# Layer 0's output projection and row norm moved into its closing step and the first MLP product; layer 1's closing step reordered

## The reference, cut to what matters

```python
# layer 0: 16 heads of 32
qn, kn, vn = LN(x, ln1), LN(ctx, ln1), LN(ctx, ln1)
out = softmax((qn @ wq + bq) (kn @ wk + bk)^T / sqrt(32)) (vn @ wv + bv)
x1  = x + out @ wo + bo
x2  = x1 + gelu(LN(x1, ln2) @ w1 + b1) @ w2 + b2          # w1: 512 x 2048
# layer 1: 16 heads of 64
out = softmax((x2 @ Wq / 8) (ctx @ Wk)^T - 2) (ctx @ Wv)
y   = LN(out @ Wfc + x2, gamma, beta)
```

## Time and profile before

| | |
|---|---|
| median of 3 runs | 1577.0 us (1571.5 to 1578.2) |
| the profiled execution | 1579.7 us, span 1577.9 us |
| TensorE (PE) busy | 1398.7 us, 89% |
| VectorE (DVE) busy | 872.8 us, 55% |
| ScalarE (ACT) busy | 694.1 us, 44% |
| GpSimd (POOL) busy | 503.5 us, 32% |
| mean granted TensorE clock | 0.951 of full |

### The profile page before, as it was taken

The page is one execution under the profiler, slowest core; times in us unless marked ns, Lnnn a source line. Parts: engine busy times, 40 slices in busy tenths (PEclk is TensorE's granted clock), DMA queues, the critical chain, the costliest instruction groups (busy, mean ns, idle before and its releaser), DMA issues. The chain is left out here.

```text
span 1577.9 us, 31349 instructions
## 1 busy us (share of the span) xinstructions
PE 1398.7 (89%) x12780; PEld 876.5 (56%) x12780; DVE 872.8 (55%) x1550; ACT 694.1 (44%) x1328; POOL 503.5 (32%) x529
## 2 busy tenths in 40 slices
PE   3864998898989856799999999999999999999996
PEld 2432565565556542454455666666666666666653
DVE  5754677677676538552343445544555555546554
ACT  4442566665565543431212444444444444444431
POOL 4701566566565657002000121111112122121122
PEclk9996999999999858899999999999999999999998
DMA  6334443443433204302344232323232232323320
GB/s 197 100 73 99 91 121 99 101 110 101 118 82 85 56 16 148 120 1 92 110 149 87 65 102 59 103 65 103 49 90 67 46 95 65 103 65 85 92 69 29
DMA packets 123985, 138.32 MB, mean 88 GB/s; under 512 B 57282, under 2 KB 99778, under 8 KB 121794
## 3 DMA queue, kind: packets, MB, share of 16 engines
q1 hardware_dynamic: 123842, 136.33, 32.6%
HBM read 61.73 MB, written 20.87 MB: 52 GB/s over the span
## 5 line engine op out<-in xcount | busy, mean ns | idle before, releaser
L608 POOL TENSOR_TENSOR attn_probs<-attn_p,attn_probs 128x400 f16<-128x400 f32 (+1 forms) x288 | 284.4, 994 | 869.9 <-ACT attn_probs L1124 866.7
L1320 DVE TENSOR_REDUCE attn_nmax<-attn_p_max 100x1 f32<-100x722 f32 x256 | 231.9, 906 | 201.9 <-PE attn_p_max L875 200.0
L858 PE MATMUL attn_p_proj<-kv_w_v,attn_ctxT 128*128 128x512 f16 (+1 forms) x1152 | 264.3, 379 | 1.1 <-DVE attn_vbuf L1359 1.1
L853 PE MATMUL attn_p_proj<-attn_ctxT,kv_w_k 128*128 128x361 f16 x1536 | 249.1, 317 | 4.1 <-DVE attn_knat L1353 3.5
L1114 ACT ACTIVATE attn_p<-attn_p_sc,attn_score_bias 128x400 f32<-128x400 f32 x192 | 113.7, 592 | 312.0 <-PE attn_p_sc L904 312.0
L1124 ACT CAST attn_probs<-attn_p 128x400 f16<-128x400 f32 (+1 forms) x384 | 197.6, 517 | 0.0
L853 PEld LDWEIGHTS attn_p_proj<-attn_ctxT,kv_w_k 128*128 128x128 f16 x1536 | 144.5, 97 | 88.7 <-DVE attn_knat L1353 9.7
L1114 ACT ACTIVATE attn_p<-attn_p_sc 128x400 f32<-128x400 f32 x192 | 96.5, 503 | 189.5 <-PE attn_p_sc L900 179.1
L858 PEld LDWEIGHTS attn_p_proj<-kv_w_v,attn_ctxT 128*128 128x128 f16 (+1 forms) x1152 | 110.3, 101 | 112.4 <-DVE attn_vbuf L1359 1.4
L858 PE MATMUL attn_p_proj<-l_w_v,attn_ctxT 128*128 128x512 f16 (+1 forms) x576 | 142.2, 400 | 0.2 <-DVE attn_kscaled L1349 0.2
L853 PE MATMUL attn_p_proj<-attn_ctxT,l_w_k 128*128 128x361 f16 x768 | 131.6, 323 | 2.1 <-DVE attn_kscaled L1349 1.9
(11 more groups left out here) (199 smaller groups left out, 2497.2 us busy)
## 6 DMA issues: line engine op xcount, KB each, us to landing
kv_w<-attn_knat SPq DMA_DIRECT2D x128, 180.5 KB, 3.4
attn_kstack<-attn_knat SPq DMA_DIRECT2D x192, 90.2 KB, 2.2
ctx_turned<-attn_ctxT SPq DMA_DIRECT2D x8, 1444.0 KB, 8.8
attn_ctxT<-ctx_turned SPq DMA_DIRECT2D x8, 1444.0 KB, 7.7
attn_kstack_b<-attn_knat SPq DMA_DIRECT2D x64, 180.5 KB, 3.6
attn_c<-in_ctx_dram SPq DMA_DIRECT2D x40, 256.0 KB
rows_wo_w<-in_L_xattn_w_dram SPq DMA_DIRECT2D x8, 512.0 KB, 3.6
cols_w_w<-in_L_xattn_w_dram SPq DMA_DIRECT2D x4, 1024.0 KB, 5.6
```

The source lines that it names most:

```text
L608: eng.tensor_tensor(probs[:r, g % 2, 1, t, :HG * SQ], p32[:r, t % 3, :], probs[:r, g % 2, 0, t, :HG * SQ], ALU.subtract).then_inc(p_lo_mad ...
L853: last = pe.matmul(bank[:, :HALF], w_k[:, wa, k, c0 + m * P:c0 + (m + 1) * P], ctxT[:, cpar, ca, k, n * HALF:(n + 1) * HALF], **flags)
L858: last = pe.matmul(bank[:r, :], ctxT[:, cpar, ca, k, P * t:P * t + r], w_v[:, wa, k, c0:c0 + E], **flags)
L1320: dve.tensor_reduce(nmax[:SQ, hh:hh + 1], p_max[:SQ, :, :HALF], AX.XY, ALU.max, negate=True).then_inc(max_made, 1)
```

## The change

- Tiles are cut alike everywhere: five of 128 rows, one of 60, one of 100 (`ROW0`, `RROWS`).
- `wo` is loaded and split one step earlier, in step 7 of layer 0; the first 512 columns of `w1` are split in the closing step into `w_first` (the room of layer 0's key weights).
- In the closing step and the tail the first five tiles go through the output projection and the row norm: `row_products` in slots 1, 7, 13, 19, 25 counted from the closing step's start, `row_sum` three slots later, then scale, shift, hi, lo, turn, one slot each. Their sums x1 are stored to memory. In the closing step the lo part of the probabilities is made by GpSimd and DVE in turn.
- `rows_stage("rows_wo")` and `columns_stage` are gone. `mlp_up` does the Gelu product with all blocks for rows 0 to 399 first, and tiles 5 and 6 on the way.
- In layer 1, `Wfc` is split in slots 4, 5, 10 and 11; `close_rows` takes slots 0 to 9; GpSimd takes the power of tile 5 in slot 9, behind `out_lo`. The first product waits for all but one of the projections to be read, the second tile for the last.

```diff
-        self.close = {1 + i: divmod(i, 2) for i in range(10)} if layer == 1 else {}
+        self.close = {i: divmod(i, 2) for i in range(10)} if layer == 1 else {}
+        self.next = [11, 12, 13, 14] if layer == 0 else [4, 5, 10, 11]
+        self.row_acc, self.row_sum, self.row_scale, self.row_add, self.row_hi, self.row_lo, self.row_turn = 1, 4, 5, 6, 7, 8, 9
+    def row_tile(self, s, j, ahead):
+        T, rest = divmod((s - self.units) * self.n + j - ahead, KT)
+        return T if self.layer == 0 and rest == 0 and 0 <= T < EARLY else None
...
 # attention, SP, layer 0
+                    if u == U - 1:
+                        sp.wait_ge(proj_ready, NPROJ * u)
+                        sp.wait_ge(ctxT_moved[0], 16 * (B // 2))
+                        load_next_weight(0)
                     stack_k(u, u % 2, 0)
...
+                for dst, vector, sem in zip((bo_row, g2_row, b2_row), mid_vectors, (bo_loaded, g2_loaded, b2_loaded)):
+                    sp.dma_start(dst, vector.partition_broadcast(P)).then_inc(sem, 16)
+                sp.wait_ge(next_lo_made, ET)
+                for T in range(EARLY):
+                    sp.dma_start(mid[T], x_d[ROW0[T]:ROW0[T] + P, :]).then_inc(mid_loaded[T], 16)
                 sp.wait_ge(proj_ready, NPROJ * U)
-                load_next_weight(0)
+                load_next_weight(1)
...
+                for T in range(EARLY):
+                    sp.wait_ge(mid_summed, T + 1)
+                    sp.dma_start(x1_d[ROW0[T]:ROW0[T] + P, :], mid[T]).then_inc(mid_stored, 16)
...
 # attention, TensorE
+            def row_products(T):
+                r0, r = ROW0[T], RROWS[T]
...
+                for k in range(ET):
+                    for i, (a, b) in enumerate(PARTS):
+                        last = pe.matmul(p_proj[:r, T % 2, :], outT[0][:, a, k, r0:r0 + r], next_weights[0][1 + b][:, k, :],
+                                         start=(k + i == 0), stop=(k == ET - 1 and i == 2))
+                last.then_inc(mid_ready, 1)
...
             def close_rows(T, half):
...
                 if T == 0 and half == 0:
                     pe.wait_ge(next_lo_made, ET * len(next_weights))
-                    pe.wait_ge(proj_freed, NPROJ * U)
+                    pe.wait_ge(proj_freed, NPROJ * U - 1)
...
+                if T == 1 and half == 0:
+                    pe.wait_ge(proj_freed, NPROJ * U)
...
 # attention, DVE
+            def row_sum(T):
...
+                dve.scalar_tensor_tensor(mid[T][:r], p_proj[:r, T % 2, :], 1.0 / WS, mid[T][:r], ALU.mult, ALU.add).then_inc(mid_summed, 1)
...
+                dve.bn_stats(stats[:r, T % 2, :], mid[T][:r]).then_inc(mid_stats_made, 1)
...
+                dve.bn_aggr(mv[:r, T, :], stats[:r, T % 2, :]).then_inc(mid_mv_made, 1)
...
+                dve.tensor_scalar(mid_rstd[:r, T:T + 1], mv[:r, T, 1:2], eps, None, ALU.add).then_inc(mid_var_made, 1)
...
+                dve.scalar_tensor_tensor(mid_z[T % 2][:r], mid[T][:r], mv[:r, T, 0:1], g2_row[:r], ALU.subtract, ALU.mult).then_inc(mid_centred, 1)
...
-                    if layer == 1 and has_scores and j > 0 and (t - 1) % 2:
+                    if (layer == 1 or s == U) and has_scores and j > 0 and (t - 1) % 2:
...
 # attention, GpSimd
-                    if layer == 1 and s == U + 1 and j == PV_T + HG:
+                    if layer == 1 and s == U + 1 and j == sl.out_t:
                         row_rstds(RT - 2)
...
+def mlp_up(nc, ident16, x_d, x1_d, xT, w_o, w_first, w, m_tiles, x1, b2_row, bias_col, scale, outT, vectors, b2_d, split, room, split_rooms):
...
+        uses = [(m, n) for n in range(2) for m in range(m_tiles)]
+        side = {0: 0, 2: 1, 5: 2, 9: 3, 13: 4, 17: 5, 21: 6}
+        sum_at, norm_at, low_at, turn_at = ({u + 2 * i: T for i, T in enumerate(late)} for u in (4, 5, 6, 8))
...
+            weight_split.load(sp, 0)
+            for T in late:
+                sp.dma_start(x1[:RROWS[T], T], x_d[ROW0[T]:ROW0[T] + RROWS[T], :]).then_inc(x_loaded[T], 16)
...
+            weight_split.load(sp, 1)
+            sp.dma_start(x1[:, :EARLY], x1_d[:P * EARLY, :].rearrange("(t p) e -> p t e", p=P)).then_inc(x1_loaded, 16)
+            sp.dma_start(b2_row[:], b2_d.partition_broadcast(P)).then_inc(b2_loaded, 16)
+            for n in range(2, len(weight_split.jobs)):
+                weight_split.load(sp, n)
...
             for u, (m, n) in enumerate(uses):
+                if u == 4:
+                    for T in late:
+                        products(T)
+                if n == 0 and m % 4 == 0 and m:
+                    pe.wait_ge(weight_split.lo_made, m // 4)
+                if n == 1 and m == 0:
+                    pe.wait_ge(turn_copied, len(late))
                 if u >= 4:
                     pe.wait_ge(made, u - 3)
...
+                if u in turn_at:
+                    turn(turn_at[u])
```

334 lines of the change are left out of this document (267 added, 67 removed).

## The result

The changed kernel takes 1561.1 us (median of 6 runs, 1558.0 to 1564.8), the kernel before 1575.1 beside it (6 runs, 1571.5 to 1578.7): ratio 0.9907, interval 0.9889 to 0.9924, some 14 us less. The forecast was 31 us less. The two profiled executions are 21.6 us apart in their spans (1577.9 and 1556.3); the profiled one of after is the fastest of its kernel's six, that of before stands 4.6 us above its kernel's median; together that explains the 7 us between the two figures.

What follows compares the result with a forecast made beforehand. TensorE bounds the projections, and stages follow strictly, so the removed stage's time is saved: -52.6 + 14 + 12 + 3 + 1 - 1.8 - 6.8 = -31 us, 1546 us from the median; range 1532 to 1565.

Steps and rivals of the forecast that it cites:

- the border argument: Between layer 0's attention and its MLP: stages follow strictly one another, so removing the output projection's stage saves its 52.6 us.
- P: Layer 0's closing step: DVE instructions with two SBUF inputs and GpSimd shut each other out, +13 us, 1559 us; chance 0.10.
- H: Layer 0's closing step and tail: clock stays down, five products at half level, 13 us more, 1559 us; chance 0.07.
- W: First MLP product: weights come late, TensorE waits 20 us and not 8, 1558 us; chance 0.06.
- Step 3: Layer 0's closing step takes four row tiles; DVE's 39 us of work at 0.8 busy make it 49 us, +12 us.
- Step 4: Layer 0's tail takes tile 4's products and row sum, +3 us; wo split in the step before, +1 us.
- rival S: Layer 0's closing step and tail: row chain not hidden, 74 us instead of 16, 1604 us; chance 0.03.
- Step 2: First MLP product takes tiles 5 and 6: products, transposes and a TensorE stall of 8 us, +14 us.
- Step 5: Layer 1's weight splits move to slots without a maximum on DVE, -1.8 us.
- Step 6: Layer 1's closing: products start one slot earlier and three TensorE or DVE waits shrink, -6.8 us together.
- (b): Layer 1's closing: DVE's last lo part no longer stands behind tile 4's row sum, -3.4 us.
- F: Layer 0's closing step: clock level stays full, matmuls and DVE's waits shorten, +3 instead of +12, 1537 us; chance 0.14.

## Why the prediction was right, and where it was not

**The sign and the range** were right, 1561 in 1532 to 1565, and the border argument held: the stage's 52.6 us went with it, and nothing took its place as a stage. That 1561 lies in the range is luck in part: its upper end stood on P, H and W, and the time went into another place than theirs. Of the signs named, the gap in the MLP stage and the end of the 1.35 us gap came; a closing step of 45 to 52 us with DVE near 0.8 and a clock above 0.8 did not (58.3 us, 0.60 and 0.76). The number was 15 us off. The profiled pair puts 13.6 us in one place and gives 4 back at small ones; the rest of the 15 is how the profiled executions stand to the medians.

**Step 3, the closing step, is the step that failed** (+12 forecast; 36.3 to 58.3 us, +22, measured). The figure 49 us was DVE's work divided by 0.8. The work was about right: 39 us with four row sums forecast, 34.8 measured with three, the fourth starting at 594.86, just behind the step. The share was the guess: 34.8 of 58.3 us are 0.60, a little under the 0.64 of the step before that I had as the far bound (which gave 61 us, so the length stayed inside the bounds). I chose between the two ends by how busy engines were, in a step where no engine's busy time sets the length.

What the runs show in its place has two parts. From the first maximum to the last it takes 14.8 us more (26.0 to 40.8). Here DVE and PE take turns over one buffer, and two row sums of 2.5 us stand in DVE's queue ahead of a maximum that PE waits for (3.51 and 3.98 us). A dose there came out as a longer gap one for one (3.51 to 4.91 us for 1.4) and as 7.9 us for 6.9 in the whole; three slots later, beside the next tile's products, the same sums cost 7.9 us less by the ratios and 7.0 by the table. From the last maximum to the last exponential it takes 7.2 us more, without any turns: PE and ScalarE wait for the row chain (4.44 us at 591.43). For this part and the tail no run takes the chain away; that it is the cause is argued, and how the +28.6 of step and tail divide between the sums' work and the chain stays open. With the sum at the better slot DVE is busy 36.9 of 51.7 us (536.4 to 588.1, 0.71), so the 0.8 was less far from what this work allows in another order.

**Step 4, the tail** (+3 forecast; 13.7 to 20.3 us, +6.6). I priced tile 4's products and sum as extras beside idle engines. In the queue tile 4's sum stands behind tile 3's lo part, which itself waits for ScalarE behind GpSimd, so two tiles' chains run one after the other: 594.86 to 602.9 and 602.80 to 612.5 us. The last times-V product stands on PE behind tile 3's transposes (602.94), and its way out, through DVE and GpSimd, behind tile 4's sum and shift; this holds PE until 609.86. A link that a row of before gave as 8.6 us was in the text, under rival S, and should have been in this sum. The +1 us for the wo split in the step before did not show: the closing step starts 1.4 us sooner. The other changed kernels, the same code up to there, have its first maximum between 535.3 and 539.1 us (537.6 before), so one pair of executions can't show 1 us.

**Step 2, the MLP stage** (+14 forecast, +12.6 measured) was right in kind: one gap, behind use 8, released by the lo part, 5.39 us for a forecast of 8; the later transposes take back 4.3 us of it. The reason differs in part. The weights were late once (ScalarE waited 4.77 us for the load at 628.20), and that was over before the gap; the piece whose split stands in front of the lo part was taken by ScalarE at 637.64 without a wait for its load. The order in DVE's and ScalarE's queues made the gap. The size is luck in part: 11 us of DVE against 6.3 and 4 us of TensorE leave under 1 us of stall and not the 4.5 of the text, which put the rest down to ScalarE's turns without a sum, and the 9.6 us of the longer working stood on late weights.

**Step 5** gave 1.5 us for 1.8. **Step 6** gave 4.6 to 5.1 us for 6.8: (a) and (c) came (gaps of 2.04 and 1.35 us gone), (b), 3.4 us, did not. I had taken it that tile 4's row sum, a slot earlier in the program, would be out of the way of the last lo part. It starts no earlier in time: in DVE's in-order queue it stands behind the lo part before it, which waited 3.28 us for ScalarE and ran at 1527.64; the sum follows until 1531.3, the last lo part at 1531.74, and PE's gap is 5.06 us for 5.03.

**The rivals.** F, the clock recovers: the granted clock rose only from 0.66 to 0.76, and the kernel with a third of the products shows that the products' time is not what the step is made of; both halves of F fall. The Trainium skill, "TensorE: Matmul & The Clock Gate" (Part 1), says that activity releases the throttle. The rows agree as to the clock (0.76 with the products, 0.65 in 536 to 594 us with a third of them), and show no gain from it that can be told in a stretch that waits. H, the half level, happened in part (2.75, 4.13, 5.32, 2.75 and 4.42 us for twelve, some 6 us in all over the full level and not 13) and cost less than can be told, for the same reason. P, the ports: DVE's lo parts took 0.703 us on average beside GpSimd for 0.570, the centring 0.751, that of the rows stage 1.313; 11 x 0.13 = 1.5 us, and with one row lo part of 1.42 us (589.95) and one weight split of 1.15 (570.18) for some 0.68 each 2.7 us, far from 13. With all lo parts on GpSimd it was some 5 us.

```profile
L744 DVE TENSOR_TENSOR attn_probs<-attn_p,attn_probs 128x400 f16<-128x400 f32 (+1 forms) x11 | 7.7, 703 | 13.0 <-ACT attn_probs L1311 13.0
...
L1613 DVE SCALAR_TENSOR_TENSOR attn_kscaled<-attn_ctxT,attn_mv,attn_c 128x512 f32<-128x512 f32 x3 | 2.3, 751 | 0.0
```

W, late weights, fell with the 5.39 us. S had the mechanism nearest to the truth, a row chain that the round doesn't hide, at 14.8 us a tile; measured are 28.6 / 5 = 5.7. Its guard, "a slot of 1.5 us lies between any two links", failed for all three engines: on DVE the row sum itself is the link in the way, TensorE waited 5.4 us for row lo parts and ScalarE 8.3 us for GpSimd's power in this step.

## What to carry to other kernels

Where two engines take turns over one buffer, price an instruction that stands in one queue ahead of the result that the other engine waits for at its full duration, whatever the busy share says; and put long side work where the other engine has long work of its own in the same turn. That the same price holds for the other engine's side work is not shown: TensorE's products here cost much less than they last. Then look in each in-order queue for the pair that cost time here at three places: the sum of one tile standing ahead of (or behind) the last small link of its neighbour. Two such moves, the row sums three slots later and what waits for the lo part four uses later, brought 12 us here, where layer 0's whole rebuilding had brought 8.

## What the runs showed beside that

The work that an experiment takes off an engine has to be read from its own trace. Instructions of 8 columns in place of 400 took 4.9 us off DVE and not the 7.5 expected, and some 4 (0 to 8) came back; 12 lo parts handed to GpSimd took nothing off DVE's busy time, since its other instructions ran longer beside them, and gave 0. And products that run at the half clock level for want of work cost less than can be told where the chain behind them waits for something else: eight of twelve matmuls left out, 2.2 to 3.4 us a tile, moved the same score product of the next group by 0.2 us, and part of the time stood as a longer wait ahead of the row tile's transposes.
